# Graph attention and feed-forward in one kernel: the exponential and the logarithm from one ScalarE table, and the one-hot comparison in two halves

## What is computed

```python
z = layernorm(x)
xp = (z @ W).reshape(n, 4, 64)                      # 4 heads of 64
a_src, a_dst = einsum(xp, att_src), einsum(xp, att_dst)
alpha = leaky_relu(a_src[src] + a_dst[dst], 0.2)     # an edge, and a loop per node
ex = exp(alpha - amax[dst]); w = ex / segment_sum(ex, dst)[dst]
x = x + elu(segment_sum(xp[src] * w, dst) + bias)
z = layernorm(x)
weights = z @ wr                                     # one score per node
sel = the best half of the nodes by weights
y = gelu(z[sel] @ w1 + b1) @ w2 + b2
out = x + z;  out[sel] += y * weights[sel]
```

## Time and profile before

| | us |
|---|---|
| median of three executions (2779.0, 2780.69, 2808.06) | 2780.69 |
| span of the profiled execution, from its first to its last instruction | 2587.4 |
| between that span and the median | 193.3 |
| of the span: the stage of the 98 windows, from the first gather to the last | 2326.5 |
| of the span: all before it, and all behind it | 156.5 and 104.4 |

### The profile page before, as it was taken

One profiled execution on the slowest core, in us unless ns is written; L12 is line 12 of the kernel. 1 busy time (PEld: TensorE's weight loads), 2 busy tenths in 40 slices (PEclk: granted clock), 3 DMA queues, 4 the chain that ended last, 5 costly groups with the idle time before them and its releaser, 6 DMA issues.

```text
span 2587.4 us, 44011 instructions
## 1 busy us (share of the span) xinstructions
PE 1983.9 (77%) x10893; PEld 1692.1 (65%) x10894; DVE 1625.5 (63%) x3934; ACT 946.1 (37%) x1960; POOL 1878.6 (73%) x1686
## 2 busy tenths in 40 slices
PE   6936787787788778877877887787778778877862
PEld 5835676666677667666766676666667667666752
DVE  5745656666666666656666666666666566666667
ACT  3512333333343333334333433434343343334330
POOL 2257777777777777777777777777777777777730
PEclk9968888898889889888998988898898899898886
DMA  7544454454455445444544544454445445444548
GB/s 251 174 122 120 133 140 123 135 140 125 134 140 138 124 134 139 135 124 136 140 125 136 140 136 123 135 138 134 124 138 140 121 135 140 134 124 136 150 135 302
DMA packets 245118, 365.39 MB, mean 141 GB/s; under 512 B 91173, under 2 KB 180417, under 8 KB 245090
## 3 DMA queue, kind: packets, MB, share of 16 engines
q0 software_dynamic: 77488, 214.85, 31.3%
q1 hardware_dynamic: 138002, 121.74, 15.3%
q10 hardware_dynamic: 29600, 28.49, 3.3%
HBM read 326.04 MB, written 38.89 MB: 141 GB/s over the span
## 4 chain that ended last, share of the span: by engine, by line
POOL 30%; PE 28%; DMA 12%; issue 11%; DVE 11%; SPq 3%; DVEq 1%; ACTq 1%; ACT 1%; POOLq 1%
POOL rows L608 30%; PE ag_ps L914 14%; DMA rows<-node_rows,srci 7%; DMA dsti<-in_dst 5%; PE h_ps L893 5%; PE y_ps L903 4%; PE ag_ps L820 3%; DVE oh L1160 3%; DVE base L1376 1%; DVEq L365 1%; SPq L365 1%; SPq L433 1%; PE tr_ps L882 1%; ACTq L771 1%; DVE rows L1192 1%
## 5 line engine op out<-in xcount | busy, mean ns | idle before, releaser
L608 POOL DMA_INDIRECT rows<-node_rows,srci x1613 | 1835.2, 1138 | 491.3 <-issue 463.6
L914 PE MATMUL ag_ps<-rows,oh 128*128 128x260 f32 x3322 | 769.0, 389 | 69.0 <-DVE rows L1192 68.8
L914 PEld LDWEIGHTS ag_ps<-rows,oh 128*128 128x128 f32 x3322 | 624.1, 192 | 189.6 <-DVE rows L1192 72.6
L903 PE MATMUL y_ps<-w2s,hT 128*128 128x256 f32 x1568 | 530.4, 499 | 7.6 <-ACT hT L709 7.6
L1192 DVE TENSOR_TENSOR rows<-rows 128x768 f32<-128x768 f32 (+2 forms) x685 | 498.9, 800 | 31.7 <-ACT rows L726 31.7
L903 PEld LDWEIGHTS y_ps<-w2s,hT 128*128 128x128 f32 x1568 | 384.8, 258 | 73.6 <-issue 7.7
L893 PEld LDWEIGHTS h_ps<-xnT,w1s 128*128 128x128 f32 x3136 | 398.9, 210 | 22.3 <-issue 18.4
L893 PE MATMUL h_ps<-xnT,w1s 128*128 128x128 f32 x3136 | 401.2, 291 | 0.5 <-ACT xnT L699 0.5
L882 PE MATMUL tr_ps<-ident,steps_of_rows 128*128 128x128 f32 x196 | 63.8, 426 | 427.1 <-DVE steps_of_rows L1263 427.1
L882 PEld LDWEIGHTS tr_ps<-ident,steps_of_rows 128*128 128x128 f32 x196 | 26.9, 193 | 465.6 <-DVE steps_of_rows L1263 465.6
L1175 DVE TENSOR_TENSOR zz<-rows,edge_dm 128x68 f32<-128x68 f32 x98 | 22.5, 229 | 455.4 <-DMA rows<-node_rows,srci 453.0
(11 more groups left out here) (169 smaller groups left out, 1504.8 us busy)
## 6 DMA issues: line engine op xcount, KB each, us to landing
dbc<-dst SPq DMA_DIRECT2D x97, 544.0 KB
rows<-node_rows,srci POOLq DMA_INDIRECT x1613, 2.8
selfr<-node_rows SPq DMA_DIRECT2D x98, 130.0 KB
base<-in_x SPq DMA_DIRECT2D x14, 896.0 KB, 5.0
base<-in_x SPq DMA_DIRECT2D x98, 128.0 KB
ffn_rows<-yb ACTq DMA_DIRECT2D x96, 128.0 KB
node_rows<-base SPq DMA_DIRECT2D x13, 910.0 KB, 5.8
out<-base SPq DMA_DIRECT2D x3, 1024.0 KB, 4.3
```

What stands on the lines that cost most here:

```text
L608: pool.indirect_dma_start(out=rows[:, b, t, :], out_offset=None, in_=table, in_offset=bass.IndirectOffsetOnAxis(ap=srci[:, b, t:t + 1], ax ...
L903: nc.tensor.matmul(y_ps[:, 0:D], hT[:, m, :], w2s[:, m, :], start=(m == 0), stop=False)
L914: nc.tensor.matmul(ag_ps[b][:, 0:ROW], oh[:, b, t, :], rows[:, b, t, :], start=(t == 0), stop=False).then_inc(tile_done, 1)
```

## The change

It sets a named table, which holds both the exponential and the logarithm, behind the eight gelu instructions of each window and once ahead of the first window. The instruction that makes oh is two instructions: the first with 8 of the 17 tiles stands where it stood, the second with 9 tiles stands behind `route`. The semaphore oh_ok counts to two per window, and its waiters are adapted.

```diff
+EXP_AND_LN = "natural_log_exp_and_others"
...
-                    wait_apart(sp, (oh_ok, w - 1), (lk_ok, w - 1))
+                    wait_apart(sp, (oh_ok, 2 * w - 2), (lk_ok, w - 1))
...
                     nc.scalar.activation(hT[:, m, :], h_ps[:, m * P:(m + 1) * P], ACT.Gelu_apprx_tanh, bias=b1s[:, m:m + 1]).then_inc(hT_ok, 1)
+                nc.scalar.preload_act_table_set(EXP_AND_LN)
...
+            nc.scalar.preload_act_table_set(EXP_AND_LN)
             exponentials(0, 0)
...
-                pe.wait_ge(oh_ok, w + 1)
+                pe.wait_ge(oh_ok, 2 * w + 2)
...
-            def one_hots(w, b):
+            def one_hots(w, b, part):
 
                 dve.wait_ge(loc_ok, w + 1)
-                n = tiles_of(w)
-                nc.vector.tensor_tensor(oh[:, b, 0:n, :], iota_d[:, :].unsqueeze(1).broadcast_to([P, n, P]),
-                                        dloc[:, 0:n].unsqueeze(2).broadcast_to([P, n, P]), ALU.is_equal).then_inc(oh_ok, 1)
+                half_of = tiles_of(w) // 2
+                first, n = (0, half_of) if part == 0 else (half_of, tiles_of(w) - half_of)
+                nc.vector.tensor_tensor(oh[:, b, first:first + n, :], iota_d[:, :].unsqueeze(1).broadcast_to([P, n, P]),
+                                        dloc[:, first:first + n].unsqueeze(2).broadcast_to([P, n, P]), ALU.is_equal).then_inc(oh_ok, 1)
...
                 if more:
-                    one_hots(w + 1, 1 - b)
+                    one_hots(w + 1, 1 - b, 0)
                 if isinstance(w, int) and w == NW - 2:
 
+                    one_hots(w + 1, 1 - b, 1)
                     exponents(NW - 1, PAIRS - 1, 1)
                 if not more:
                     residual(w, i, b)
                 if known(w, 1):
                     route(w - 1, 1 - b)
+                if not isinstance(w, int) or w < NW - 2:
+                    one_hots(w + 1, 1 - b, 1)
 
             one_hots_turned(0, 0, 0)
-            one_hots(0, 0)
+            one_hots(0, 0, 0)
+            one_hots(0, 0, 1)
```

## The result

The changed kernel took 2991.91 us (median of four runs, 2969.54 to 3039.59) against 2784.94 us (2779.0 to 2808.06) for the kernel before in the same comparison: ratio 1.0677, 95% interval 1.0618 to 1.0737. The times given are medians of all executions, while a ratio goes by the undisturbed ones of each kernel, up to 1.5% above its fastest. The forecast was 2727 us, faster. It was wrong, by 265 us and in the sign.

A forecast was written before the change was run, and what follows sets the result against it. GpSimd's unbroken gathers were taken to bound the kernel, stretched by VectorE's comparison. Span 2587.4 - 55 (shorter stalls) + 1.3 (behind the last window) = 2533.7, with 193.3 us around it 2727 us; range 2685 to 2765.

The forecast's parts named there:

- What bounds the kernel: GpSimd's gathers, issued one behind another without semaphore waits, fill the window stage: 1835.2 us busy, 491.3 us idle.
- slower: Rival: both comparison halves meet a gather at their start, stalls 2.305 us against 1.93; 2818 us, chance 0.08.
- The stalls: Gathers held by VectorE's comparison: 0.71 plus 0.645 us a window instead of 1.93, 55 us less in all.
- The rival of a VectorE held by a gather: Second half waits for a running gather, stall 0.92 us, gain only 29 us: 2753 us; chance 0.05.
- The tables: Two of four ScalarE loads a window go, 2.57 us, worth nothing themselves; rs0 comes earlier, so `route` starts at once.
- the tail: Behind the last window, an added table load ahead of gelu delays it: +1.3 us.
- the second load covered: Behind the last window, the next added load has 1.70 us and the wait ahead as cover: costs nothing.
- my first rival: Second half starts over 0.7 us later, a gather slips past: 107 us saved, 2675 us; chance 0.12.

The follow-up runs named there:

- a pause: Changed kernel plus one dummy GpSimd operation of 2.0 us behind gather 9 of each window: 2695.35 us (before 2589.78); on another chip 2832.78 us (before 2793.15).
- the chip of the account: Changed kernel unchanged, run again beside the kernel before on one chip: 2991.99 us against 2782.99, ratio 1.0739.
- the split alone: Kernel before with the comparison in two instructions, four table loads a window kept: 2467.08 us (ratio 0.9559); on another chip 2932.41 us (1.047).
- back to back: Changed kernel with the second half directly behind the first, ahead of the normalisation: 2456.02 us, ratio 0.952 to the kernel before; repeated 2457.15 us.

## Why the prediction was wrong, by its own steps

**What bounds the kernel: the step that failed.** "GpSimd never stands still for a semaphore" was true of the trace I read and of every other of its kind without a pause (idle 491.3 to 491.6 us), and I made the sum for another population: the 2780.69 us of the runs shown. The difference of 193.3 us I took over as a constant "around" the span. On chips where before takes 2785 us it is stops of GpSimd inside the span, 220 us in 55 stops over 1 us on the chip of the account. So the step put at nothing a wait of GpSimd for TensorE's product L917, for which 499.7 us stand in the run of the comparison. The number was in front of me: one execution 7% under the median of the others is not overhead, it is another behaviour, and it deserved a rival. None of my four rivals had TensorE's release come late; "slower" had 0.07, by two stalls in full, which no run showed.

**The stalls** held, on the chips of the first kind. The changed kernel there, in the place of the earlier trace rows:

```profile
1309.81 1.23 DVE L1164 TENSOR_TENSOR oh<-iota_d,dloc 128x1024 f32<-128x1024 f32 x1
1310.59 1.27 POOL L609 DMA_INDIRECT rows<-node_rows,srci  x1 [0.30 <-issue]
1312.03 0.43 DVE L1269 TENSOR_TENSOR base<-base,steps_of_rows 128x256 f32 x1
1312.16 1.12 POOL L609 DMA_INDIRECT rows<-node_rows,srci  x1 [0.30 <-issue]
1313.01 1.35 DVE L1164 TENSOR_TENSOR oh<-iota_d,dloc 128x1152 f32<-128x1152 f32 x1
1313.58 1.59 POOL L609 DMA_INDIRECT rows<-node_rows,srci  x1 [0.30 <-issue]
```

The first half ends at 1311.04 and its gather at 1311.86, 0.82 behind. The second half starts at E + 1.97 (forecast 1.98), and its gather takes 1.59 us, a stall of 0.645, the forecast to the last digit. Over all windows the first stall is 0.62 us (forecast 0.71) and the second 0.64; the halves take 1226 and 1349 ns (forecast 1210 and 1345):

```profile
L1164 DVE TENSOR_TENSOR oh<-iota_d,dloc 128x1152 f32<-128x1152 f32 x97 | 130.8, 1349 | 0.0
L1164 DVE TENSOR_TENSOR oh<-iota_d,dloc 128x1024 f32<-128x1024 f32 x97 | 118.9, 1226 | 1.1 <-issue 1.1
```

The term was forecast at -55 us. On these chips the gathers' busy time is 1829.5 less 1766.9 = 62.6 us shorter (from one chip to another), and the time 66.5 us (on one): the term was about 10 us too small, because the gather's place in the first half did move: it starts 0.77 to 0.80 us into it in 34 windows, where I took 20. The forecast's 54 us would be 2.1% there, and 2.5% were measured.

The rival of a VectorE held by a gather falls with the same rows: the second half began at 1313.01 under the gather of 1312.16 to 1313.28 and took its usual 1.35 us, as did all 97 of them (1.347 to 1.353). The Trainium skill (SBUF — State Buffer, "SBUF: two separate sides") has the side that starts first block the other; no row here shows a comparison that was blocked, only gathers.

**The tables** by themselves: 2582.09 against 2580.51 us, nothing, with +1.3 us forecast for the tail. The load there does stand in the path, behind a wait of 1.68 us for TensorE that doesn't cover it:

```profile
2465.46 1.28 ACT L710 ACT_TABLE_LOAD   x1 [1.68 <-PE h_ps L896]
```

There I had called the second load covered; its part is within what the comparison can tell. But the tables aren't neutral beside the split. In the split alone the exponential still waits for its load, and the second half comes later:

```profile
1304.64 1.23 DVE L1162 TENSOR_TENSOR oh<-iota_d,dloc 128x1024 f32<-128x1024 f32 x1
1304.95 1.28 ACT L765 ACT_TABLE_LOAD   x1
1306.48 0.22 DVE L1255 SCALAR_TENSOR_TENSOR sq<-rs,vareps 128x1 f32<-128x1 f32 x1 [0.61 <-ACT rs L765]
1308.53 1.35 DVE L1162 TENSOR_TENSOR oh<-iota_d,dloc 128x1152 f32<-128x1152 f32 x1
1309.49 1.21 POOL L609 DMA_INDIRECT rows<-node_rows,srci  x1 [0.31 <-issue]
```

It starts at E + 2.66, 0.7 us later than in the changed kernel, and the next gather starts 0.96 us into it: stall 0.27 instead of 0.64. That is my first rival (0.7 us later, and a gather slips past), and it is what the split alone does: 2467 us against 2523 with the tables, on chips where before takes 2580.51 and 2589.78. Taking out a load that was off the path cost 1.9% by the two ratios, some 49 us, and 54.6 us by the gathers' busy time (1766.9 against 1712.3), since it moved a comparison onto a gather. On these chips the change is worth 2.5%, and back to back 4.8%: there the second half starts 0.08 us ahead of the first one's end, and the stalled gather is let go between the two.

```profile
1299.31 2.49 DVE L1164 TENSOR_TENSOR oh<-iota_d,dloc 128x1024 f32<-128x1024 f32 x2
1299.75 1.60 POOL L609 DMA_INDIRECT rows<-node_rows,srci  x1 [0.30 <-issue]
1301.66 0.97 POOL L609 DMA_INDIRECT rows<-node_rows,srci  x1 [0.30 <-issue]
```

The first half ends near 1300.54, and the gather at 1301.35, 0.81 behind it, though the second half runs till 1301.80. The next one starts 0.14 us ahead of that and meets only the end.

**Why the gain turned into a loss** on the other chips. Shown: the busy time falls there too (-73.5 us); the idle time grows by 271 us, in stops that come when GpSimd has used up its buffers while the others' updates are late; a break of 2 us in the row of gathers ends the lateness in 37 of 56 windows. Why the change brings more of these, I can't show. My first thought was that the one comparison of before was such a break: it held up a gather for up to 2.13 us in each window, and the halves do it for 1.18 us at most (2.124 less 0.945); so the change would have taken away the breath the other engines used. The 8 late copies of before on the chip of the account against 50 of the changed kernel seem to say so. The wider count takes most of that away: before has 67 updates over 5 us late there against 144, most of them at gelu instead of the copy; none of the 67 arrived in one of its 88 gathers of over 2 us, and none was due when such a gather began. So the long hold released no such update there. It doesn't settle what a shorter hold does to a shorter lateness: of the 36 updates there that came 3 to 5 us late, 27 arrived in gathers of 1.3 to 2 us. And whether a hold puts off the start of a late stretch isn't shown.

What stays open: what begins a late stretch, and why on some chips only. Three chips besides that of the comparison were of this kind, five were not. No chip was met a second time, so that it is the chip, and not its state at the time, isn't shown either. And back to back, the fastest version, was never run on a chip where before takes 2785 us; the split alone, next to it in kind, was slower there by 4.7%. So I name no version as better than the kernel before on all chips.

## What to carry to other kernels

When the profiled execution and the median of the timed runs differ by several per cent, find out where the difference sits before you forecast; a sum made on the quick execution holds for its kind only. On the bounding engine, ask how many buffers it has until a late release reaches it (here GpSimd ran on for 23 us, and then stopped for 14): time taken off its own work turns into waiting if the others don't keep up. Count lateness at every wait and not at one, since it moves from one place to another. And where one engine issues on a fixed grid, the place of a disturbance counts as much as its length: 0.7 us of shift was worth some 50 us.

## What the runs showed of the hardware

- On some chips, while GpSimd issued gathers one behind another, a finished matmul's update reached ScalarE up to 29.1 us late (split alone) and VectorE up to 28.1 us (changed kernel), and SyncE took some 0.71 us for a DMA issue of 0.33 us. The gathers kept their 0.945 us. About half of the changed kernel's late copies (27 of 51, 26 of 50) came 2.2 to 3.9 us behind the last gather before a stop, and 37 of 56 came 0.8 to 5.1 us behind the start of a pause of 2 us.
- On the other chips no window before the tail had such a late copy, none of 1195 recorded updates in seven traces came over 3 us late, and GpSimd had no stop over 1 us that wasn't a pause put in.
- The mean granted TensorE clock of the profiled executions was 0.87 to 0.91 on the first kind of chip and 0.82 to 0.83 on the second, the kernel before showing 0.883 in 2581.0 us and 0.832 in 2797.6 us; whether that is a cause or a consequence isn't told apart.
- A gather held by a VectorE comparison ends 0.82 us behind the end of that comparison, and 0.81 us behind it where the next one follows directly.
